# Attention tables of a four-layer graph network: order of ScalarE's copies, waits for loads

## What is computed

```python
k = typed_matmul(h, k_linears, node_type)          # one of 4 weights by the node's type; so q and v
q_att = einsum('nhd,rhde->rnhe', q, relation_att)  # 8 relations, 4 heads of 64
v_msg = einsum('nhd,rhde->rnhe', v, relation_msg)
score = sum(q_att[etype, col_idx] * k[row_idx], -1) * (relation_pri[etype] / 8)
alpha = segment_softmax(score, col_idx)
agg = segment_sum(alpha[..., None] * v_msg[etype, row_idx], col_idx)
```

## Time and profile before

| what | us |
|---|---|
| median of 3 runs | 4201.42 (4199.71 to 4203.07) |
| the profiled execution, device time | 4203.95 |
| its span, first to last instruction | 4202.1 |
| TensorE busy | 3172.8 (76%) |
| GpSimd busy | 2744.3 (65%) |
| VectorE busy | 2231.3 (53%) |
| ScalarE busy | 894.9 (21%) |
| granted TensorE clock, mean | 0.841 of full speed |

### The profile page before, as it was taken

How to read it: one execution, slowest core, us unless ns; L and a number is a source line. 1 busy time by engine, 2 the same in 40 slices (tenths; PEclk the granted TensorE clock), 3 DMA queues, 4 the chain that set the end, 5 groups by cost and what they waited for, 6 DMA issues and landing times. The chain is left out here.

```text
span 4202.1 us, 64286 instructions
## 1 busy us (share of the span) xinstructions
PE 3172.8 (76%) x11666; PEld 2176.1 (52%) x11666; DVE 2231.3 (53%) x7567; ACT 894.9 (21%) x2584; POOL 2744.3 (65%) x2879
## 2 busy tenths in 40 slices
PE   5999938877788873886888878888886777676764
PEld 2444426666566642333676767777544444444442
DVE  8200047666666645344888857766663443433435
ACT  1333300000200000441444555555320000100000
POOL 3777767777677774334777747777317777477774
PEclk9999969889899986997878768777898877888776
DMA  4333323333333334566555535555313333333332
GB/s 141 141 148 146 145 71 105 106 106 105 95 106 106 106 107 145 224 246 231 165 164 165 165 94 161 163 162 163 82 46 105 105 105 105 99 105 106 106 105 90
DMA packets 226896, 540.00 MB, mean 129 GB/s; under 512 B 73482, under 2 KB 107948, under 8 KB 212876
## 3 DMA queue, kind: packets, MB, share of 16 engines
q0 software_dynamic: 136528, 374.97, 30.3%
q1 hardware_dynamic: 57880, 103.46, 6.8%
q10 hardware_dynamic: 32164, 57.91, 4.6%
HBM read 390.04 MB, written 146.09 MB: 128 GB/s over the span
## 5 line engine op out<-in xcount | busy, mean ns | idle before, releaser
L579 POOL DMA_INDIRECT gcn_edges_g<-table,rows_i x782 | 741.1, 948 | 429.4 <-ACTq L844 191.8
L892 PE MATMUL ps<-gcn_edges_g,gcn_edges_onehot 128*128 x1760 | 627.6, 496 | 308.5 <-SPq L590 274.5
L937 DVE TENSOR_TENSOR acc<-acc,ps 128x256 f32 (+1 forms) x880 | 369.4, 420 | 751.9 <-PE ps L892 740.4
L892 PEld LDWEIGHTS ps<-gcn_edges_g,gcn_edges_onehot 128*128 128x128 f32 x1760 | 391.0, 242 | 537.6 <-issue 484.3
L305 POOL DMA_INDIRECT records<-rec,slots x391 | 376.2, 962 | 184.7 <-issue 124.0
L579 POOL DMA_INDIRECT sum_g<-table8v,rows_i x391 | 379.7, 971 | 163.0 <-issue 112.2
L579 POOL DMA_INDIRECT rel_g<-table,rows_i x391 | 372.1, 952 | 135.0 <-issue 96.9
L579 POOL DMA_INDIRECT score_g<-table8k,rows_i x391 | 371.3, 950 | 135.1 <-issue 112.7
L579 POOL DMA_INDIRECT conv_edges_g<-table,rows_i x391 | 371.6, 950 | 127.4 <-issue 93.8
L357 PE MATMUL ps<-w,xt 128*128 128x512 f32 x1000 | 435.8, 595 | 18.3 <-ACT xt L327 18.3
L1016 PE MATMUL ps<-q,onehot_t 128*128 x880 | 320.5, 500 | 113.2 <-DVE onehot_t L1114 111.9
(11 more groups left out here) (315 smaller groups left out, 4778.5 us busy)
## 6 DMA issues: line engine op xcount, KB each, us to landing
table<-tb SPq DMA_DIRECT2D x50, 1280.0 KB, 4.5
score_dst_bc<-dst_rows ACTq DMA_DIRECT2D x110, 256.0 KB, 3.5
sum_dst_bc<-dst_rows ACTq DMA_DIRECT2D x110, 256.0 KB, 3.5
gcn_edges_g<-table,rows_i POOLq DMA_INDIRECT x782
table<-gcn_tb SPq DMA_DIRECT2D x50, 128.0 KB, 1.7
records<-rec,slots POOLq DMA_INDIRECT x391
rel_g<-table,rows_i POOLq DMA_INDIRECT x391
conv_edges_g<-table,rows_i POOLq DMA_INDIRECT x391
```

Source lines behind the costliest of these rows:

```text
L579: pool.indirect_dma_start(out=m.g[:, 2 * (p % RING) + j, 0:D], out_offset=None, in_=table, in_offset=bass.IndirectOffsetOnAxis(ap=m.rows_i ...
L892: mm = pe.matmul(bank(m, i % BANKS, 0, width), m.onehot[:, 2 * k + j, :], window(m.g, slot + j, 0, width), start=(j == 0), stop=(j == 1))
L937: nc.vector.tensor_tensor(acc, acc, bank(m, i % BANKS, 0, width), ALU.add).then_inc(added, 1)
```

## The change

Three edits. In `attention_tables`, ScalarE's loop copies k and v of the next group (`keep_kv(i + 1)`) ahead of the table copies of group i, and its copy of `kvt` and `pick` change places. Each of the five parts of `xs` is waited for at the first group that may need it, in place of all five ahead of the first. SyncE no longer waits for the load of `m.q`; a semaphore that lives on past the block (`m.q_back`) is waited for by TensorE at the start of `attention_scores`.

```diff
@@ attention_scores @@
         def _(pe):
             regs = ItemRegisters(pe, m, "score")
+            pe.wait_ge(m.q_back, 16)
             for i in range(total):
@@ attention_tables @@
             for b in (0, 1):
                 sp.wait_ge(q_slots[b], 16 * (G // 2))
-            sp.dma_start(m.q[:, 0:NT, :], m.q_rows[0:ROWS, :].rearrange("(t p) d -> p t d", p=P)).then_inc(q_stored, 16)
-            sp.wait_ge(q_stored, 16)
+            sp.dma_start(m.q[:, 0:NT, :], m.q_rows[0:ROWS, :].rearrange("(t p) d -> p t d", p=P)).then_inc(m.q_back, 16)
             for j in (0, 1):
                 sp.wait_ge(stored[j], 16 * G)
             sp.wait_ge(m.bias_in, 48)
@@ attention_tables, ScalarE @@
             def pick(i):
                 if i < G:
+                    if i < NT and i % PART == 0:
+                        act.wait_ge(back[i // PART], 16)
                     if i >= 2:
                         act.wait_ge(turned, i - 1)
                     copy(xc[:, i % 2, :], window(xs, act.snap(regs[i % 3], min_val=0, max_val=NT - 1))).then_inc(picked, 1)
 
+            def keep_kv(i):
+                if i < G:
+                    act.wait_ge(typed, i + 1)
+                    if i >= 2:
+                        act.wait_ge(kv_turned, i - 1)
+                    copy(kv[:, i % 2, :], bank(m, 1, 0, 512)).then_inc(kv_ready, 1)
+
             for i in range(3):
                 load(i)
-            for b in range(5):
-                act.wait_ge(back[b], 16)
             pick(0)
             pick(1)
+            keep_kv(0)
             for i in range(G):
-                pick(i + 2)
-                load(i + 3)
-                act.wait_ge(typed, i + 1)
-                if i >= 2:
-                    act.wait_ge(kv_turned, i - 1)
-                copy(kv[:, i % 2, :], bank(m, 1, 0, 512)).then_inc(kv_ready, 1)
                 act.wait_ge(kv_turned, i + 1)
                 if i >= 2:
                     act.wait_ge(product, 8 * (i - 1))
                 copy(kvt[:, i % 2, :, :], bank(m, 3, 0, 512).rearrange("p (c n) -> p c n", c=4)).then_inc(kvt_ready, 1)
+                pick(i + 2)
+                load(i + 3)
+                keep_kv(i + 1)
                 to_table(act, copy, i, 1, odd)
```

More of the change, by code:

```diff
@@ L1639, in attention_tables @@
          marks_flat, marks_found, into_ready, rel_ready, picked, turned, xt_ready, typed, kv_ready, q_ready, kv_turned, kvt_ready,
-         product, even, odd, att_turned, q_stored) = sems(
+         product, even, odd, att_turned) = sems(
             ctx, nc, "att", "weights_in", "rel_in", "chain", "dis_summed", "dis_rooted", "joined", "back0", "back1",
             "back2", "back3", "back4", "marks_turned", "marks_flat", "marks_found", "into_ready", "rel_ready", "picked", "turned",
-            "xt_ready", "typed", "kv_ready", "q_ready", "kv_turned", "kvt_ready", "product", "even", "odd", "att_turned",
-            "q_stored")
+            "xt_ready", "typed", "kv_ready", "q_ready", "kv_turned", "kvt_ready", "product", "even", "odd", "att_turned")
         placed, stored, q_slots = m.placed, m.stored, m.q_slots
@@ L1648, in attention_tables @@
                     marks_found, into_ready, rel_ready, picked, turned, xt_ready, typed, kv_ready, q_ready, kv_turned, kvt_ready,
-                    product, even, odd, att_turned, q_stored]
+                    product, even, odd, att_turned]
         block = ctx.enter_context(nc.Block())
@@ L2102, in four_graph_layers @@
         m.scattered = sems(ctx, nc, "all", "scattered0", "scattered1")
-        m.marked, m.placed = sems(ctx, nc, "all", "marked", "placed")
+        m.marked, m.placed, m.q_back = sems(ctx, nc, "all", "marked", "placed", "q_back")
         m.stored = sems(ctx, nc, "all", "stored_k", "stored_v")
```

## The result

The changed kernel takes 4182.41 us, median of 6 runs (4177.63 to 4187.65), against 4200.69 (4198.14 to 4203.07, 6 runs) for the kernel before on the same chip. The ratio is 0.9957, 95% interval 0.9944 to 0.997: 18.3 us faster, where 30.8 were forecast, and 2.4 us above the upper end of the range. The direction was right and so was edit 1. Edit 2 worked as forecast but was priced too high, and edit 3 removed a wait that ended only 1.2 us after the next one.

A forecast was written before the change was run, and what follows sets the result against it. It took the first pick, TensorE's group loop with a 1.58 us hole, and the wait for q as bounds; 6.8 + 23.4 - 4.9 + 5.5 = 30.8 us gave 4170.6 us from the median, range 4164 to 4180.

The forecast's parts named there:

- edit 1: Ahead of the first group: xs parts waited for singly, first pick at 1671.8 instead of 1678.58, 6.8 us gained.
- Edit 2: Group loop: next group's k and v copied first, period 8.92 to 8.02 us; 23.4 less 4.9, so 18.5 us.
- edit 3: Block's end: only TensorE waits for q, GpSimd's first gather at 1945.7 instead of 1951.23, 5.5 us gained.
- first sign: Group loop: the prediction counts as wrong if the period stays over 8.3 us.
- With 0.05 us to react (as `turn_back` does after 1774.85): Group loop: by_type starts 0.05 us after the copy of q ends, at 1774.50 instead of 1775.40.
- The late stores: Group loop: v landings longer than the room, 5.78 us instead of 6.68, stall VectorE's copies; 4.9 us charged back.
- The block now ends with the last landing of v, 1944.6, in place of 1950.2: Block's end: v's last landing instead of q's ends the block, first gather following by 1.03 us; 5.5 us gained.
- The lower bound, 0: Block's end and score stage: least gain allowed for moving the wait for q; bounds 0 and 6.5 us.
- Rival B: Score stage: q comes so late that consumers keep the lag, q's moved wait worth 0 to 1; 4175.4 us, chance 0.12.
- Rival D: Score stage: later wait keeps TensorE at half clock, 0.70 us per item, up to 154 us, 4324; chance 0.03.
- Rival A: Group loop: v's stores become the bound, period at least landing + 2.24; at 6.2 landing 8.44, 4176.6 us; chance 0.13.
- Rival C: Group loop: long landings fall into the slack, k and v copy move brings 22.5, sum 34.8, 4166.6 us; chance 0.12.

The follow-up runs named there:

- e1_parts: Kernel before with only the parts of xs waited for singly, each at the first group that may need it: 4196.07 us, ratio 0.9988.
- f4_static: Changed kernel with by_type's weights always taken from type 0 at a fixed address, on a slower chip: 5430.70 us, ratio 0.9964 to the kernel before.
- g2_qcopy: Changed kernel with VectorE's copy of q of the next group also ahead of its table copies: 4154.87 us, ratio 0.9888 to the kernel before.
- e3_q: Kernel before with only the wait for the load of q moved from SyncE to TensorE at the score stage's start: 4199.50 us, ratio 0.9997.
- g3_qlast: Changed kernel with the load of q issued only after the last stores have landed: 4177.72 us, ratio 0.994 to the kernel before.
- g4_both: Changed kernel with VectorE's q copy ahead of its table copies and q's load behind the last stores: 4150.45 us, ratio 0.988 to the kernel before.
- e2_loop: Kernel before with only ScalarE's copy of the next group's k and v ahead of its table copies: 4189.20 us, ratio 0.9976.
- e4_after: The changed kernel, all three edits, timed again beside its parts against the kernel before: 4181.76 us, ratio 0.9953.
- g1_after: The changed kernel timed again on another chip, as base for later variants: 4183.75 us, ratio 0.9954 to the kernel before.
- f2_qlast: Changed kernel with q's load issued only after the last stores have landed, on a slower chip: 5425.94 us, ratio 0.9958 to the kernel before.

## Why the prediction was off, step by step

By its own first sign, a period that stays over 8.3 us, the prediction is wrong: it is 8.32.

**Edit 1: right.** Forecast 6.8 us. The pick came 4.39 us after the first load was issued, for the 4.5 forecast. The gain at the copy of k and v was 6.4 in the changed kernel, 6.0 in e1_parts and 7.0 between the means of all ten traces; e1_parts' time gives 5.3 (1.3 to 8.8 by its interval).

**Edit 2: mechanism right, price wrong.** The hole ahead of `turn_back` closed, `by_type` waits for the copy of q, and the order of the rest is as before. The step that failed is "With 0.05 us to react (as `turn_back` does after 1774.85)", and with it "From there on the order is as before, so the period is 8.92 - 0.90 = 8.02 us". `turn_back` has fixed addresses, and its queue has no entry between wait and weight load. `by_type` takes its weights by a register, and its queue works out that address behind the wait. In the kernel before this work lay under `turn_back`'s matmuls, so the earlier trace rows show it nowhere. f4_static prices it at 0.10 to 0.12 us. A second part, some 0.05, stands in the trace and was taken out by no run: the wait has an entry of its own on the queue, 51 ns long, in f4_static too. The third is 0.10 from the start of `by_type` to `by_relation` (2.99 for 2.89). The first weight load, which started 0.11 us ahead of the first matmul before, now starts with it, and that matmul takes 692 ns for 595. In g2_qcopy, without a wait, the load is 0.11 us ahead again and the matmul back at 595 ns. So the period is 8.32, some 0.03 to 0.05 of it without a cause, and 26 periods give 26 x 0.60 = 15.6 us, not 23.4.

The late stores were charged 4.9 us. From `by_type(1)` to `by_type(27)` it was 232.55 us before and is 220.19 after, a gain of 12.4, so stalls took 15.6 - 12.4 = 3.2 us. That term was right in kind and a little large, because the period shrank less: the prediction's own count, with 6.08 us of room in place of 5.78, gives 4.9 - 2.0 = 2.9. (Its count at 5.78, 6.9, should read 7.1.) Over the traces the loss to late stores varies more than that, from 0.6 to 4.2 us without edit 2 and from 3.9 to 7.9 with it; the means differ by 3.3. So the close agreement of the one pair is partly luck. Edit 2 forecast 18.5 and gave 12.2 in the time and 12.25 in the trace: 6 of the 12.5 us by which the forecast missed, and just inside the bounds of 12 to 23.4.

**Edit 3: one arrival read, two there.** Forecast 5.5 us, measured 1.9 in the time, 1.33 in e3_q's trace and 1.29 in the changed kernel's. The step that failed is "The block now ends with the last landing of v, 1944.6, in place of 1950.2". I had taken SyncE to be the last at the block's end. The row said otherwise: the first gather's bracket in the earlier trace rows names POOLq L1619, GpSimd's own queue at the block's end, after 16.25 us, and not SyncE. It should have been looked up by that line. It shows the drain until 1949.2, and with it a bound of 1.2 us for whatever happens to q, as long as v lands when it does. The lower bound, 0, covered this; the value taken did not.

**What the later wait does: hardly tried by the change, no loss where it was.** Rival B feared a late q. The forecast had GpSimd start some 7 us ahead of q's arrival, and q slowed by the gathers. In the changed kernel q landed 0.08 us after the first gather, 17.5 us after its issue for 17.6, so there was no lead that could be lost, and TensorE's first matmul did not wait for q. There TensorE starts 3.75 us after the first gather (3.40 before, 1954.63 - 1951.23) and the last gather comes 490.06 us after the first (489.14 before, 2440.37 - 1951.23). Only the kernels with q held back try the rival, with TensorE some 10 us behind the first gather, and g3_qlast and g4_both show no loss beyond the spread. Rival D, a lower clock for longer, did not come: between first and last gather the granted clock was 0.79 before, 0.78 after and 0.80 in g3_qlast.

**Rival A's floor was 0.3 us too high.** It held the period to v's landing + 2.24 = 7.54 us. g2_qcopy runs at 7.28 with a usual landing of 5.3, since copies that waited run back to back and the issue follows in 1.94. A floor of landing + 1.9 is there: where a landing took 7.16 us, the next store was issued 9.03 us after the last. Rival C, whose reason this was, had part of it right (held copies catch up), but the added stalls of 3.2 us were no smaller than the count gives, and `by_type`'s start-up cost 7.8 us more.

**The sum, remade** with the sizes that the trace shows: 6.4 + 15.6 - 3.2 + 1.3 = 20.1 us, which is 0.4, 6.1 and 4.2 short of the forecast in its three edits, against 18.3 (12.6 to 23.5 by its interval), 19.7 and 17.8 measured in three sets of runs.

## What to carry to other kernels

When a wait disappears, price the next one with the instruction that will stand behind it, register work in its queue included; a row of another instruction that reacts in 0.05 us isn't its price. Before a wait at a block's end is taken away, list the arrival of every engine there, GpSimd's drain too: what can be gained is the distance to the second latest, here 1.2 us of 17. And when a copy that frees a bank is moved forward, move its twin on the other engine as well: the second half of the same idea (g2_qcopy) was worth 28.9 us where the first gave 12.2.

## What the hardware showed unexpectedly

- GpSimd's drain at the block's end is not a fixed cost. It lasted 15.4 us before, 15.2 after and 10.1 in g3_qlast, and ended 4.49 us after the last landing of its stores in each of the traces before, after, e1_parts, e2_loop, e3_q, e4_after, f4_static, g1_after and g2_qcopy (landings of 10.0 to 11.4 us, drains of 14.7 to 16.1), but 5.3 in three without q's load alongside, f2_qlast, g3_qlast and g4_both, where it lasted 10.1 us. Whether it then follows the landing or has reached a least length, and what it does in these microseconds, no run shows.
- The last store of v, 1 MB, landed after 10.5 us with the load of q issued 1.5 us ahead of it, and after 4.6 us when q was held back until it was down. The Trainium skill (DMA: Bandwidth & Descriptors, Issuing engines are not separate DMA queues) says that transfers of different engines share the same 16 DMA engines; these two numbers agree with it. The load of q itself took 17.5 us beside the store and 16.0 behind it.
- Address work on TensorE's queue behind a wait cost about 0.1 us a group, once nothing lay over it, and a first weight load that no longer ran ahead of its matmul another 0.1.
- `by_type(0)`, the first real work after a pause, took 4.58 us before, 5.05 after and 5.48 in e1_parts, against 2.75 to 2.84 in the loop. It varies with the clock and not with the edit: its granted clock was 0.62, 0.56 and 0.50 in these three, and 0.50 over 5.48 us in e2_loop, which feeds TensorE as late as before. TensorE had been idle for 29 to 38 us ahead of it in each.
- The chip that took 5451 us for the kernel that others did in 4201 granted less clock: 0.74 over the span for 0.84. In f2_qlast the group loop had 1.00 and its usual period of 8.32 us, and the score stage 0.65 and 640 us for 0.78 and 490 in the changed kernel. What lowered the clock there no run shows.
- Left open: the last 0.03 to 0.05 us of the changed kernel's period, and the drain's length past the landing.
